# A sooner token list, and gathers in another order on GpSimd's queue, in a sorted feed-forward stage

## The chip, the cores and the metric

The kernel runs on one core of a Trainium2 chip. The metric is the device time of one execution in microseconds; below it is the median of three runs. A profile of one further execution stands beside it. Engines are named as the profile names them: PE is TensorE, DVE is VectorE, ACT is ScalarE, POOL is GpSimd, SP is the engine that issues plain transfers.

## What is computed

Four layers work on 2048 tokens of width 256 (8 sequences of 256). The change lies in the second, a hard-routed feed-forward. Each token walks down a binary tree of depth 8 and ends in one of 256 leaves; the leaf has its own small weights. Products q, k and v do this three times, with trees and weights of their own, on the same tokens:

```python
def _fff(x, nw, nb, w1, b1, w2, b2, act):
    node = jnp.zeros(x.shape[:2], dtype=jnp.int32)
    for _ in range(DEPTH):
        logit = jnp.einsum('bsd,bsd->bs', x, nw[node]) + nb[node]
        node = 2 * node + 1 + (logit > 0).astype(jnp.int32)
    leaf = node - NN
    h = act(jnp.einsum('bsd,bsdl->bsl', x, w1[leaf]) + b1[leaf])
    return jnp.einsum('bsl,bsld->bsd', h, w2[leaf]) + b2[leaf]

q = _fff(xn, q_nw, ...)
k = _fff(xn, k_nw, ...)
v = _fff(xn, v_nw, ...)
```

An attention over q, k and v, a fourth such product, and the other layers follow.

## The kernel before, in words

The function `group_products` handles q, k and v in one call (`nf` is 3, product number `f` is 0, 1, 2). It has two parts.

**Routing.** 24 items (8 blocks of 256 tokens for q, then for k, then for v) pass through a loop of 26 steps, `i` from 0 to 25, written out on PE and DVE. In step `i` PE computes the logits of item `i` (`pe_logits`, L1607), the leaf sums of item `i-1` (`pe_follow`, L1617) and the look-up of item `i-2` (`pe_look_up`, L1628). DVE turns logits into sides (`dve_sides`, L1567) and takes the look-up's result (`dve_take`). When a product's eight items are through, its tokens are sorted by leaf: `count` and `rank` on PE, `starts`, `slots`, `locate` on DVE, `find_tokens` on PE (L2209, it waits for the two halves of `is_row`, L2018), and `found_tokens` on DVE (its last instruction is L2034), which sets the semaphore `found_in`. From then on there is a list of the 2048 tokens in order of their leaves, and the row of the bias table for each. The step numbers at which q's pieces run are literals in the two loops (B is 8). `steps`, `words_of` and `pack` make the bits that say at which unit the group of leaves changes.

**Products.** The sorted tokens are 16 tiles of 128 (NT is 16), the leaves 32 groups of 8. A product is 47 units (UNITS), one for each pair of tile and group that can meet. A tile `t` is brought from the DRAM tensor `rows_x` by an indirect DMA on POOL's queue (`gather`, L1765) into one of six buffers (RING), is transposed by PE (`turn`, L2145 and L2147), and is copied by ACT to `xT`. A unit is `hidden` (L2158), ACT's activation, DVE's `leaf_only` (L2041), `output` (L2168), and DVE's `add` (L2060). The first `add` on a tile adds to rows of biases that another indirect DMA has put there (`seed`, L1778). In unit `u` PE does `turn` of tile `u+3` first; the turns of the next product's tiles 0 to 2 are done in units 44 to 46. So 16 turns lie in the first part of each product, and the last 34 units of each have none.

**POOL's queue.** POOL issues the gathers and seeds in program order and waits in that order. A gather of the `n`th tile in all (`n` is `16*f + t`) waits until turn `n-6` is done, because its buffer is that tile's, and until gather `n-2` has landed. A seed waits until the seed two before it has landed, and, for the third product, until the first product's tile has been stored. The order before is: six gathers, sixteen seeds, ten gathers for q; then for k and v each sixteen seeds and sixteen gathers.

**SP's queue.** While product `f` runs, SP loads the weights of product `f+1`, a pair of groups as the old pair is no longer needed (from unit 17 to the last), and stores each finished tile of product `f` (L1811, units 31 to 46). So SP's transfers are thickest at the end of q's and of k's units.

Of the kernel before, what the change touches and what calls it, by code (L numbers as in the profile page):

```python
# [1655 lines left out]
def group_products(core, name, first, nf, leaves, weights, places, rows, beside, gelu=False,  # L1656
# [5 lines left out]

    nc = core.nc
    RING = 6 if nf > 1 else NT
    HALF_K = 0.5 * (P - 1)
    with ExitStack() as own:
        def sb(n, shape, dt=F32):
# [85 lines left out]
        with nc.Block() as block:  # L1753
            @block.gpsimd
            def _(pool):
                def gather(f, t):

                    n = f * NT + t
                    if t == 0:
                        pool.wait_ge(found_in, f + 1)  # L1760
                    if n >= RING:
                        pool.wait_ge(x_ps, n - RING + 1)
                    if n >= 2:
                        pool.wait_ge(tile_in[(n - 2) % RING], 16 * ((n - 2) // RING + 1))
                    pool.indirect_dma_start(  # L1765
                        xs[n % RING][:], None, core.rows_x if route else core.rows_f,
                        bass.IndirectOffsetOnAxis(token_i[:, f, t:t + 1], 0)
                        ).then_inc(tile_in[n % RING], 16)

                def seed(f, t):  # L1770

                    if f == 1 and t == 0:
                        pool.wait_ge(route.G_sb, route.ITEMS)
                    if f > 1:
                        pool.wait_ge(stored[t], 16 * (f - 1))
                    if t >= 2:
                        pool.wait_ge(seeded[t - 2], 16 * (f + 1))
                    pool.indirect_dma_start(  # L1778
                        ys[f % 2][:, t * D:(t + 1) * D], None, core.dram["group_b2"],
                        bass.IndirectOffsetOnAxis(leaf_row[:, f, t:t + 1], 0)  # L1780
                        ).then_inc(seeded[t], 16)

                pool.iota(column_i[:], pattern=[[1, P]], base=0, channel_multiplier=0
                          ).then_inc(column_in, 1)
                if route:
                    route.pool(pool)
                    pool.wait_ge(route.rows_out, 16 * B)
                    for t in range(RING):
                        gather(0, t)
                    for t in range(NT):  # L1790
                        seed(0, t)
                    for t in range(RING, NT):
                        gather(0, t)
                    for f in range(1, nf):
                        for t in range(NT):
                            seed(f, t)
                        for t in range(NT):
                            gather(f, t)
                else:
                    pool.wait_ge(core.rows_out, 16 * B)  # L1800
                    for t in range(NT):
                        gather(0, t)
                    for t in range(NT):
                        pool.wait_ge(tile_in[t], 16)
                    beside.pool_ahead(pool)
# [95 lines left out]
            def _(dve):  # L1901
# [5 lines left out]
                def starts(f, k):  # L1907

                    if k == 0:
                        dve.wait_ge(counted, f + 1)  # L1910
                        dve.tensor_copy(run[0][:, LOW + 1:], psZ[:, 0:NG8 - 1]
                                        ).then_inc(count_in, 1)
                        dve.wait_ge(count_in, f + 1)
                    for n in ((0, 1), (2, 3, 4))[k]:
                        old, new = run[n % 2], run[1 - n % 2]
                        by = 1 << n
                        do(dve.tensor_tensor(new[:, LOW:], old[:, LOW:],
                                             old[:, LOW - by:LOW - by + NG8], ALU.add))
# [104 lines left out]
                def found_tokens(f):  # L2023

                    dve.wait_ge(found_ps, f + 1)
                    found = psZ[:, 0:3 * NT].rearrange("p (k t) -> p k t", k=3)
                    do.mark(dve.tensor_copy(sorted_leaf[:, f], found[:, 2]))
                    do(dve.tensor_copy(tile_row[:, 0], found[:, 0]))
                    do.mark(dve.tensor_tensor(token_i[:, f], tile_row[:, 0], found[:, 1], ALU.add))
                    do.mark(dve.tensor_tensor(  # L2030
                        leaf_row[:, f], sorted_leaf[:, f],
                        leaves.offset[:, first + f:first + f + 1].to_broadcast([P, NT]), ALU.add))
                    do.wait()
                    dve.tensor_copy(tile_row[:, 1, 0:1], tile_row[:, 0, 0:1]).then_inc(found_in, 1)  # L2034
# [29 lines left out]
                if route:  # L2064
                    route.dve_first(dve, do)
                    number_tokens()
                    for i in range(route.ITEMS + 2):
                        if i + 2 < B:
                            route.dve_normal(dve, i + 2)
                        if i < route.ITEMS:  # L2070
                            route.dve_sides(dve, i)
                        if i >= 2:
                            route.dve_take(dve, do, i - 2)
                        if i == B + 3:
                            starts(0, 0)
                        if i == B + 4:
                            starts(0, 1)
                        if i == B + 5:
                            slots(0, 0)
                        if i == B + 6:  # L2080
                            slots(0, 1)
                        if i == B + 7:
                            locate(0, 0)
                        if i == B + 8:
                            locate(0, 1)
                        if i == B + 9:
                            steps(0, 0)
                        if i == B + 10:
                            found_tokens(0)
                        if i == B + 11:  # L2090
                            steps(0, 1)
                        if i == B + 13:
                            pack(0)
                        if i == 2 * B + 3:
                            starts(1, 0)
                        if i == 2 * B + 4:
                            starts(1, 1)
                        if i == 2 * B + 6:
                            slots(1, 0)
                        if i == 2 * B + 7:  # L2100
                            slots(1, 1)
                        if i == 2 * B + 8:
                            locate(1, 0)
                        if i == 2 * B + 9:
                            locate(1, 1)
                else:
                    for k in range(2):
                        starts(0, k)
                    number_tokens()
                    for k in range(2):  # L2110
                        slots(0, k)
                    for k in range(2):
                        locate(0, k)
                    found_tokens(0)
                    for k in range(2):
                        steps(0, k)
                    pack(0)
# [18 lines left out]
            def _(pe):  # L2136
# [94 lines left out]
                if route:  # L2231
                    route.pe_turn(pe, 0)
                    for i in range(route.ITEMS + 2):
                        if i < route.ITEMS:
                            route.pe_logits(pe, i)
                        if i + 1 < B:
                            route.pe_turn(pe, i + 1)
                        if 1 <= i <= route.ITEMS:
                            route.pe_follow(pe, i - 1)
                        if i >= 2:  # L2240
                            route.pe_look_up(pe, i - 2)
                        if i == B + 3:
                            count(0)
                            rank(0)
                        if i == B + 9:
                            find_tokens(0)
                        if i == B + 12:
                            words_of(0)
                        if i == 2 * B + 3:
                            count(1)  # L2250
                        if i == 2 * B + 5:
                            rank(1)
                else:
                    count(0)
                    rank(0)
                    find_tokens(0)
                    words_of(0)
# [1371 lines left out]
```

## Time and profile before

| what | us |
|---|---|
| median of 3 runs | 1495.77 (1494.61 to 1495.92) |
| the profiled execution's own time | 1499.22 |
| its span in the profile | 1497.4 |
| PE busy in the span | 1241.3 |
| POOL busy in the span | 446.6 |
| first turn of q to last unit of v, about | 545 to 763 |

Times of the rows below are microseconds from the span's start. "Idle before" is the idle time of that engine just before an instruction, and behind the arrow is what ended it, as far as the profile shows; "issue" means nothing that it shows.

### The profile page before, as it was taken

Reading aid. Unit: us, or ns where it says so; the run is one execution under the profiler, and the core shown is the slowest. Engines: PE = TensorE matmul, PEld = TensorE weight load, DVE = VectorE, ACT = ScalarE, POOL = GpSimd, SP = SyncE. Lnnn points to the kernel's source line nnn. Section 1 sums busy time; section 2 is a strip of 40 time slices with the busy share of each in tenths; the row PEclk is TensorE's granted clock in tenths of the full one; section 3 lists DMA queues with packets and bytes.
Section 4 is the critical chain, followed back from the end, with each engine's and each line's share of the span. In section 5 each row is a group of like instructions: output and inputs, shape, how many; then the busy total and the mean of one; then the engine's idle time right before and its main releaser. Section 6 shows DMA issues by size and latency. Waiting matters only on the chain. (4 is left out here: it accounts for less than half of the span.)

```text
span 1497.4 us, 24672 instructions
## 1 busy us (share of the span) xinstructions
PE 1241.3 (83%) x7232; PEld 900.6 (60%) x7236; DVE 885.1 (59%) x2513; ACT 582.4 (39%) x1106; POOL 446.6 (30%) x588
## 2 busy tenths in 40 slices
PE   1298999999875866888957758779999889999997
PEld 1195777777664755666646636556676555555554
DVE  8998999999514654645533455554656424453534
ACT  2124556665421224465632316344555541212110
POOL 2258344544461055243225416432111000000000
PEclk9658999999988988998977879887999989999999
DMA  9000000000003623759154505630100000000000
GB/s 274 0 2 2 1 1 1 1 1 1 1 1 60 245 74 92 232 162 299 48 174 146 177 27 117 157 81 8 16 9 8 1 1 0 15 0 14 0 15 14
DMA packets 85380, 92.70 MB, mean 62 GB/s; under 512 B 19400, under 2 KB 70090, under 8 KB 85260
## 3 DMA queue, kind: packets, MB, share of 16 engines
q1 hardware_dynamic: 72972, 66.05, 14.0%
q0 software_dynamic: 12288, 25.18, 6.8%
q8 instruction: 60, 0.98, 0.3%
q14 instruction: 60, 0.49, 0.1%
HBM read 76.51 MB, written 14.68 MB: 61 GB/s over the span
## 5 line engine op out<-in xcount | busy, mean ns | idle before, releaser
L3350 ACT ACTIVATE m_silu<-m_psG 128x512 f32<-128x512 f32 x48 | 28.7, 597 | 215.2 <-PE m_psU L3470 215.2
L2158 PE MATMUL gq_psH<-gq_xT,gq_w 128*128 (+1 forms) x564 | 101.1, 305 | 10.7 <-ACT gq_xT L1852 3.7
L3403 DVE TENSOR_TENSOR m_act<-m_silu,m_psU 128x512 f32<-128x512 f32 x48 | 33.0, 688 | 122.4 <-ACT m_silu L3350 107.7
L2158 PEld LDWEIGHTS gq_psH<-gq_xT,gq_w 128*128 128x128 f32 x564 | 80.9, 205 | 37.6 <-issue 32.9
L2041 DVE SCALAR_TENSOR_TENSOR gq_hT<-gq_xT,unit_leaf,gq_act 128x128 f32<-128x128 f32 x141 | 49.7, 352 | 78.5 <-ACT gq_act L1873 36.7
L2168 PE MATMUL gq_psY<-leaf_w,gq_hT 128*128 (+1 forms) x282 | 90.9, 405 | 6.2 <-DVE gq_hT L2041 4.3
L3470 PE MATMUL m_psG<-m_xnT,m_gate 128*128 128x512 f32 x192 | 91.8, 601 | 2.1 <-PEq L192 2.1
L3470 PE MATMUL m_psU<-m_xnT,m_up 128*128 128x512 f32 x192 | 90.8, 595 | 0.0
L1765 POOL DMA_INDIRECT gq_x<-rows_x,gq_token_i x48 | 46.0, 958 | 127.6 <-DVE gq_tile_row L2034 61.9
L765 DVE MATCH_REPLACE8 s_product_a_rest<-a_top,s_product_a_rest 128x256 f32<-128x256 f32 x192 | 76.1, 408 | 0.3 <-issue 0.3
L2764 ACT ACTIVATE c_probT<-c_psA 128x2048 f32<-128x2048 f32 x32 | 60.1, 1878 | 33.2 <-PE c_psA L3058 33.2
L205 POOL TENSOR_SCALAR m_rstd<-m_mean_var 128x4 f32<-128x4 f32 x4 | 0.9, 231 | 240.2 <-DVE m_mean_var L1297 240.2
L2060 DVE TENSOR_TENSOR gq_y<-gq_psY,gq_y 128x256 f32 (+1 forms) x141 | 59.6, 423 | 21.9 <-PE gq_psY L2168 13.4
L2867 DVE TENSOR_REDUCE c_max<-c_psA 128x4 f32<-128x1024 f32 x32 | 39.2, 1226 | 49.6 <-PE c_psA L3024 49.6
L3482 PE MATMUL m_psD<-m_down,m_act 128*128 128x256 f32 x256 | 60.9, 381 | 7.1 <-DVE m_acc L3428 7.1
L3428 DVE SCALAR_TENSOR_TENSOR m_acc<-m_psD,m_weight,m_acc 128x256 f32<-128x256 f32 x128 | 53.1, 478 | 22.3 <-PE m_psD L3482 22.3
L755 DVE MAX8 a_top<-s_product_a_rest 128x8 f32<-128x256 f32 x192 | 64.9, 411 | 2.0 <-DVE s_product_a_rest L765 0.5
L1873 ACT ACTIVATE gq_act<-gq_psH,leaf_b 128x128 f32<-128x128 f32 x141 | 51.4, 365 | 36.8 <-PE gq_psH L2158 22.6
L3470 PEld LDWEIGHTS m_psU<-m_xnT,m_up 128*128 128x128 f32 x192 | 36.9, 192 | 46.7 <-issue 46.7
L3482 PEld LDWEIGHTS m_psD<-m_down,m_act 128*128 128x128 f32 x256 | 48.1, 190 | 25.6 <-issue 14.2
L1058 PE MATMUL a_psW<-s_tables_a_work,a_w 128*128 128x256 f32 x256 | 60.6, 393 | 2.7 <-ACT s_tables_a_work L663 2.7
L1865 ACT ACTIVATE gq_w<-leaf_w 128x256 f32 (+1 forms) x141 | 58.2, 413 | 4.7 <-issue 4.3
(545 smaller groups left out, 3093.0 us busy)
## 6 DMA issues: line engine op xcount, KB each, us to landing
leaf_w<-in_group_w SPq DMA_DIRECT2D x128, 128.0 KB
leaf_w<-in_group_w SPq DMA_DIRECT2D x64, 256.0 KB
a_w<-in_L_xattn_W SPq DMA_DIRECT2D x2, 1024.0 KB, 12.9
rows_x<-token_rows SPq DMA_DIRECT2D x8, 256.0 KB, 5.1
sorted_y_q<-gq_y SPq DMA_DIRECT2D x16, 128.0 KB
sorted_y_k<-gq_y SPq DMA_DIRECT2D x16, 128.0 KB
sorted_y_v<-gq_y SPq DMA_DIRECT2D x16, 128.0 KB
rows_f<-token_rows SPq DMA_DIRECT2D x8, 256.0 KB
```

Of the source, the lines that this page charges most:

```text
L755: do.mark(dve.max(top[:, j, 8 * r:8 * r + 8], row_in(r, j)))
L765: last = dve.match_replace(rest[:, j, :], top[:, j, 8 * r:8 * r + 8], row_in(r, j), NEG_TAKEN)
L1058: last = pe.matmul(pW[:, 2 + c // 2 % 2, c % 2, :], w1[:, k, c * P:(c + 1) * P], hT[:, k, :], start=(k == 0), stop=(k == DC - 1))
L1865: act.activation(w1[n % 3][:], weights.w1[:, :, bass.ds(g * P, P)], ACT.Copy).then_inc(w_sb, 1)
L1873: act.activation(act_h[n % 2][:], psH[n % 2][:, 0:P], ACT.Gelu if gelu else ACT.Relu, bias=weights.b1[:, first + f, bass.ds(g, 1)]).then_i ...
L2060: dve.tensor_tensor(here, psY[n % 3][:, 0:D], here, ALU.add).then_inc(y_sb, 1)
L2158: last = pe.matmul(psH[n % 2][:, 0:P], w1[n % 3][:, c, :], xT[:, c, bass.ds(g * -P + u * P, P)], start=(c == 0), stop=(c == DC - 1))
L2168: pe.matmul(psY[n % 3][:, 0:D], hT[n % 2][:], weights.w2[:, bass.ds(g * D, D)], start=True, stop=True).then_inc(y_ps, 1)
L2764: act.activation(probT[c][:], psA[:], ACT.Exp, scale=float(DH1) ** -0.5).then_inc(exps.s, 1)
L3428: last = dve.scalar_tensor_tensor(acc[:, t, :], psD[:, t, :], wt[:, t, e:e + 1], acc[:, t, :], ALU.mult, ALU.add)
L3470: last = pe.matmul(o[u % 2][:], w[:, u, c, :], xnT[:, c, :], start=(c == 0), stop=(c == DC - 1))
L3482: last = pe.matmul(psD[:, t, :], act_u[u % 2][:, t * P:(t + 1) * P], down[:, u, :], start=True, stop=True)
```

## The change

Two things are done. First, q's sorting pieces are put at earlier routing steps and closer together: `count` and `rank` at step B+2 (was B+3) and before that step's look-up, both parts of `starts` at B+2, of `slots` at B+3 and of `locate` at B+4 (were B+3 to B+8, one a step), `find_tokens` at B+5 (was B+9), `found_tokens` at B+6 (was B+10), `steps` at B+7 and B+8, `words_of` at B+9, `pack` at B+10.

Second, POOL's order is the same for each product now: six gathers, nine seeds, then gather and seed by turns (gathers 6 to 12, seeds 9 to 15), then gathers 13 to 15. Every gather or seed waits for the one issued two before it, of whichever kind.

```diff
+    SEEDS = 9
...
-                    if n >= 2:
-                        pool.wait_ge(tile_in[(n - 2) % RING], 16 * ((n - 2) // RING + 1))
+                    if len(under_way) >= 2:
+                        pool.wait_ge(*under_way[-2])
+                    under_way.append((tile_in[n % RING], 16 * (n // RING + 1)))
...
-                    if t >= 2:
-                        pool.wait_ge(seeded[t - 2], 16 * (f + 1))
+                    pool.wait_ge(*under_way[-2])
+                    under_way.append((seeded[t], 16 * (f + 1)))
...
-                    for t in range(RING):
-                        gather(0, t)
-                    for t in range(NT):
-                        seed(0, t)
-                    for t in range(RING, NT):
-                        gather(0, t)
-                    for f in range(1, nf):
-                        for t in range(NT):
+                    for f in range(nf):
+                        for t in range(RING):
+                            gather(f, t)
+                        for t in range(SEEDS):
                             seed(f, t)
-                        for t in range(NT):
+                        for t in range(SEEDS, NT):
+                            gather(f, t - SEEDS + RING)
+                            seed(f, t)
+                        for t in range(NT - SEEDS + RING, NT):
                             gather(f, t)
...
+                        if i == B + 2:
+                            starts(0, 0)
+                            starts(0, 1)
                         if i == B + 3:
-                            starts(0, 0)
+                            slots(0, 0)
+                            slots(0, 1)
                         if i == B + 4:
-                            starts(0, 1)
-                        if i == B + 5:
-                            slots(0, 0)
+                            locate(0, 0)
+                            locate(0, 1)
                         if i == B + 6:
-                            slots(0, 1)
+                            found_tokens(0)
...
+                        if i == B + 2:
+                            count(0)
+                            rank(0)
                         if i >= 2:
                             route.pe_look_up(pe, i - 2)
-                        if i == B + 3:
-                            count(0)
-                            rank(0)
+                        if i == B + 5:
+                            find_tokens(0)
                         if i == B + 9:
-                            find_tokens(0)
-                        if i == B + 12:
                             words_of(0)
```

## Rows read from the trace of the kernel before

**Rows 1.** The page's first line.

```profile
span 1497.4 us, 24672 instructions
```

**Rows 2.** Stretch, length; PE, PEld, DVE, ACT, POOL busy us; PEclk, DMA share, GB/s.

```profile
545.10:582.00 36.90, 25.24 (x150) 19.43 (x151) 13.61 (x44) 13.74 (x38) 22.17 (x23) 0.81 0.27 83
634.60:662.00 27.40, 22.29 (x139) 16.95 (x137) 10.71 (x31) 15.81 (x45) 12.43 (x13) 0.99 0.54 170
694.70:730.30 35.60, 27.79 (x141) 19.83 (x141) 11.43 (x32) 16.06 (x46) 14.75 (x16) 0.86 0.58 183
```

**Rows 3.** PE's waits from 500 to 775 us: total, times, longest.

```profile
PE gq_psX L2145 <- DMA gq_x<-rows_x,gq_token_i: 15.1, 9, 8.9
PE gq_psX L2145 <- issue: 9.1, 6, 5.4
```

**Rows 4.** PE's timeline: start, length, line, operation, turns, and k's last output.

```profile
545.09 0.66 PE L2145 MATMUL gq_psX<-identity,gq_x 128*128 128x128 f32 x2 [2.85 <-issue]
...
581.14 0.38 PE L2145 MATMUL gq_psX<-identity,gq_x 128*128 128x128 f32 x2
...
634.64 0.38 PE L2145 MATMUL gq_psX<-identity,gq_x 128*128 128x128 f32 x2
...
640.60 0.38 PE L2145 MATMUL gq_psX<-identity,gq_x 128*128 128x128 f32 x2
...
661.36 0.48 PE L2145 MATMUL gq_psX<-identity,gq_x 128*128 128x128 f32 x2
...
694.11 0.63 PE L2168 MATMUL gq_psY<-leaf_w,gq_hT 128*128 x2
700.11 0.66 PE L2145 MATMUL gq_psX<-identity,gq_x 128*128 128x128 f32 x2 [5.36 <-issue]
...
729.57 0.44 PE L2145 MATMUL gq_psX<-identity,gq_x 128*128 128x128 f32 x2 [0.60 <-DMA gq_x<-rows_x,gq_token_i]
```

**Rows 5.** POOL's timeline: seeds of q, gathers of q, gathers of k.

```profile
553.04 0.94 POOL L1778 DMA_INDIRECT gq_y<-in_group_b,gq_row_leaf  x1 [0.80 <-DMA gq_y<-in_group_b,gq_row_leaf]
...
555.94 0.94 POOL L1778 DMA_INDIRECT gq_y<-in_group_b,gq_row_leaf  x1 [0.70 <-DMA gq_y<-in_group_b,gq_row_leaf]
...
569.89 0.94 POOL L1765 DMA_INDIRECT gq_x<-rows_x,gq_token_i  x1 [2.66 <-DMA gq_x<-rows_x,gq_token_i]
...
573.35 0.95 POOL L1765 DMA_INDIRECT gq_x<-rows_x,gq_token_i  x1 [1.27 <-PE gq_psX L2147]
...
635.40 0.95 POOL L1765 DMA_INDIRECT gq_x<-rows_x,gq_token_i  x1 [17.02 <-PE gq_psX L2147]
...
641.63 0.94 POOL L1765 DMA_INDIRECT gq_x<-rows_x,gq_token_i  x1 [4.03 <-PE gq_psX L2147]
...
648.06 0.94 POOL L1765 DMA_INDIRECT gq_x<-rows_x,gq_token_i  x1 [3.92 <-PE gq_psX L2147]
```

**Rows 6.** Busy time by stretch, around the first gathers of k's ring.

```profile
636.00:648.00 12.00, 10.20 (x68) 8.00 (x65) 5.61 (x16) 7.54 (x23) 3.18 (x4) 1.00 0.82 286
648.00:656.00 8.00, 7.10 (x44) 5.38 (x45) 2.83 (x8) 5.22 (x15) 4.85 (x5) 1.00 0.23 66
```

**Rows 7.** Routing: DVE's busy time in three plain steps, and in five with q's list.

```profile
496.70:503.80 7.10, 7.10 (x50) 6.03 (x49) 4.17 (x18) 2.06 (x3) 0.00 (x0) 1.00 1.06 375
504.90:521.10 16.20, 14.47 (x104) 11.91 (x102) 14.39 (x54) 4.16 (x7) 0.00 (x0) 1.00 0.43 149
```

**Rows 8.** Routing: timelines of PE (logits), DVE (the list's end) and SP (last `rows_x`).

```profile
509.25 1.97 PE L1607 MATMUL gq_psH<-gq_y,gq_xT 128*128 128x256 f32 x8
...
521.40 3.61 PE L1607 MATMUL gq_psH<-gq_y,gq_xT 128*128 128x256 f32 x8
...
525.44 1.97 PE L1607 MATMUL gq_psH<-gq_y,gq_xT 128*128 128x256 f32 x8
...
527.01 0.15 DVE L2034 COPY gq_tile_row<-gq_tile_row 128x1 f32<-128x1 f32 x1
...
508.10 0.43 SPq L1500 DMA_DIRECT2D rows_x<-token_rows  x1
```

More of the change, by code:

```diff
@@ L1755, in _ @@
             def _(pool):
+                under_way = []
                 def gather(f, t):
@@ L2073, in _ @@
                             route.dve_take(dve, do, i - 2)
+                        if i == B + 2:
+                            starts(0, 0)
+                            starts(0, 1)
                         if i == B + 3:
-                            starts(0, 0)
+                            slots(0, 0)
+                            slots(0, 1)
                         if i == B + 4:
-                            starts(0, 1)
-                        if i == B + 5:
-                            slots(0, 0)
+                            locate(0, 0)
+                            locate(0, 1)
                         if i == B + 6:
-                            slots(0, 1)
+                            found_tokens(0)
                         if i == B + 7:
-                            locate(0, 0)
+                            steps(0, 0)
                         if i == B + 8:
-                            locate(0, 1)
-                        if i == B + 9:
-                            steps(0, 0)
+                            steps(0, 1)
                         if i == B + 10:
[L2089 to L2092, printed above, removed]
                             pack(0)
```

## The prediction

> **What bounds the kernel now.** I read the page's first line for the span [rows 1], then PE's waits, then busy time by stretch, then the timelines of PE and POOL. The products follow each other on PE, and what comes after them waits for v's last unit, so a microsecond gained or lost on PE in the products moves the end by as much. In the 218 us of the products PE's largest wait is for gathered tiles: 15.1 us in nine waits, and 9.1 us more that the profile puts down to nothing but which lie at the same instruction, the first transpose of a turn [rows 3]. All of that is in the part of each product that has turns. These parts, from first to last turn, are the three stretches of [rows 2]. PE is busy 25.2 of 36.9 us in q's, 22.3 of 27.4 in k's, and 27.8 of 35.6 in v's. The last 34 units of each product have no turns and don't depend on POOL. So I cost the change by three windows and move the rest bodily. A window runs from when PE could begin turn 0 to the start of turn 15 [rows 4]:
>
> q: 581.14 - 545.09 = 36.05. k: 661.36 - 634.64 = 26.72. v: PE is through with what precedes at 694.11 + 0.6 = 694.7 and waits 5.36 us, so 729.57 - 694.7 = 34.9. Together 97.7 us. A window has 16 turns; k's, the shortest, gives 1.8 us a turn, so PE could hardly do any of them in less than 26 us.
>
> **What the change does to a window.** Before, q's window contained the last seeds and ten gathers, k's only ten gathers, because k's sixteen seeds had been issued while q's turnless units ran, in time that POOL otherwise idles: it waits 17.02 us before k's gather 6 [rows 5]. Now gather 6 of a product can't be issued before that product's turn 0 is done (its buffer), and seven seeds stand behind it in the queue, each ahead of the next gather. So each window now contains 17 POOL transfers, ten gathers and seven seeds, and PE's turns 7 to 15 wait for them. No instruction is added or removed on any engine; the waits and the order are all.
>
> POOL's chain in a window is then: gather 6 about 0.9 us after turn 0 begins (k's: 635.40 against 634.64, [rows 4, 5]); from a gather to the next one is one pair, gather and seed, and the next gather waits for the last one's landing; from gather 6 to 13 are seven pairs, from 13 to 15 one more; gather 15 needs about 3.0 us to reach PE (estimate: the landing time of the pairs below). With p for a pair: 0.9 + 8p + 3.0.
>
> What p is: two transfers are in flight at once, so a pair lasts from one issue to its landing. Two seeds in quiet time: 555.94 - 553.04 = 2.9, 2.95 in the mean of the neighbours. Two gathers in quiet time: 573.35 - 569.89 = 3.46 [rows 5]; other late gathers show the same. I take 3.2, in the middle, since both kinds go by turns now; the ends are 2.95 and 3.46. Near the start of k's window a pair is much longer: 641.63 - 635.40 = 6.2 and 648.06 - 641.63 = 6.4. The profile names PE as the releaser of both, but the turns that these gathers need are 2 and 4 of k, and even turn 4 was done by 641.3 (it began at 640.60, [rows 4]); what came last was the landing of the gather two before. That is SP's burst: the DMA engines are 0.82 busy from 636 to 648, at 286 GB/s, and 0.23 from 648 to 656 [rows 6]. The burst is tied to the last units of the product before, so it stays where it is relative to turn 0, for k and for v. Before, ten gathers could bear two slow pairs: PE had tiles 0 to 5 in hand and the two pairs served tiles 6 to 9. Now the two slow pairs bring only tiles 6 and 7.
>
> The Trainium skill (DMA: Bandwidth & Descriptors, section Latency and other measured facts) gives the memory's latency as 0.2 us in the mean and 2 us at high load, a dominant part of a transfer's fixed cost. The trace agrees in direction, and shows more: 6.2 against 3.46 us. By the page's 1.8 us on top of 3.2 the two slow pairs would be 5.0 each, and the sum below would be +0.7 instead of +5.9.
>
> **q.** Window 0.9 + 8 x 3.2 + 3.0 = 29.5 us; SP is silent here, so no slow pair. The sooner list is what lets six gathers and nine seeds (15 x 1.5 = 22.5 us at two in flight) be out of the way by turn 0. Before, it was ready at 527.01 [rows 8], too late for that. Now: the list needs 14.39 - 5 x 4.17/3 = 7.4 us of DVE [rows 7], and 7.4 us in three PE steps of 2.36 us (7.1 us for three in the plain stretch, [rows 7]), of which plain routing takes 1.39 each, is 4.5 us too much. `find_tokens` stands on PE one step behind `locate` and waits for it, with the logits of the next item behind it. Before, the same meeting cost 521.40 - (509.25 + 4 x 2.36 = 518.7) = 2.7 us, and 1.6 us for logits at half the clock after it (3.61 against 1.97) [rows 8]. So PE comes out of routing about 2 us later than before, with 0 and +4 as ends; the list comes at about 519 to 520, and the rows of tokens in DRAM, last issued at 508.10, are long there. 520.5 + 22.5 = 543 is ahead of turn 0 at 547. If PE's loss were hidden the term would be 0; nothing lies over it, since PE paces routing.
>
> **k.** 0.9 + 6.2 + 6.4 + 6 x 3.2 + 3.0 = 35.7. **v.** The same, and 0.7 more: six gathers after k's last turn and nine seeds under SP's loads take about as long as k's 34 turnless units (33.3 us), so gather 6 may come 0 to 1.5 us late. 36.4. The 5.36 us before v's turn 0 are gone in return, since v's first gathers are no longer behind sixteen seeds; that is inside the 34.9 of before.
>
> **Sum.** 2.0 + 29.5 + 35.7 + 36.4 = 103.6 against 97.7: +5.9 us. By window: q -4.5, k +9.0, v +1.5. With p at 2.95: 2.0 + 27.5 + 34.2 + 34.9 = 98.6, +0.9; at 3.46: 2.0 + 31.6 + 37.3 + 38.0 = 108.9, +11.2. The windows were read in an execution that took 1499.22 us with a span of 1497.4; the median of the runs shown is 1495.77, and I put the difference on that: 1501.7.
>
> **Rivals.** *The burst does not meet POOL's chain.* POOL issues nothing now between its fifteen early transfers and k's gather 6; SP's loads may drain further ahead, and all pairs be 3.2. For it: in 648 to 656 the engines are at 0.23. Against it: 286 GB/s in the 12 us where the slow pairs lie come from SP's own stores and loads [rows 6]. Then 2.0 + 29.5 + 29.5 + 30.2 = 91.2, -6.5, 1489.3: faster. It decides when a slow pair costs under 1.5 us more than a quiet one, about half of what was read.
>
> *One slow pair a window instead of two*, if the burst is shorter by some 4 us: 2.0 + 29.5 + 32.5 + 33.2 = 97.2, -0.5, 1495.3: no change. For it: fewer of POOL's own transfers are in the engines before it.
>
> *Worse.* p at 3.46, a third slow pair (+3 in k and v), routing +4: 4 + 31.6 + 40.3 + 41.0 = 116.9, +19; or PE, waiting in every turn, falls to its lower clock for the units behind a window, as for the logits at 521.40 [rows 8]. Half of this is likelier than all: 1507 to 1512.
>
> *It doesn't do what it says*: the list is sooner but the first turn isn't, as turn 0 waits for all of routing. That is so, and is in the sum; a sooner list alone gives nothing but room for the seeds.
>
> **How the numbers follow.** Forecast 0.47, by itself 1496.7 to 1507; one slow pair 0.17; no slow pair 0.18; worse 0.18. About 0.2% (3 us) is what a measurement of this kernel can tell from no change. Slower: 0.18 and all but 0.05 of 0.47, 0.60. Same: 0.17 + 0.05 = 0.22. Faster: 0.18. The range reaches from the better case to the milder half of the worse: 1490 to 1508.
>
> **What would show it.** Right: `found_in` near 519; turn 0 of q at 547; turn 15 of q 27 to 32 us later; k's turn 15 34 to 37 us behind its turn 0 (was 26.7), with waits for gathered tiles from turn 7 on; no wait of 5 us before v's turn 0; two pairs over 5 us on POOL after turn 0 of k and of v. Wrong: k's window under 32 us, or a pair p outside 2.9 to 3.5 in quiet time, or seeds late enough that DVE's `add` waits.

## The result, and the profile after

The changed kernel takes 1506.65 us (median of six runs, 1501.25 to 1512.45), the kernel before 1495.19 beside it (six runs, 1490.16 to 1499.56). The ratio is 1.0079, 95% interval 1.0049 to 1.0108: slower, by 11.5 us between the medians. The profiled execution of the changed kernel is its fastest, 1501.25 us, so its span is only 2.0 us over [rows 1]:

```profile
span 1499.4 us, 24679 instructions
```

The loss has to be looked for in the products, and there it is whole. PE's timeline after, the turns that answer to [rows 4] (turn 0 and 15 of q, then k's turn 0, 6, 7 and 15, then v's turn 0, 6 and 15):

```profile
545.07 0.66 PE L2145 MATMUL gq_psX<-identity,gq_x 128*128 128x128 f32 x2 [2.69 <-DVE token_rows L1577]
...
579.18 0.38 PE L2145 MATMUL gq_psX<-identity,gq_x 128*128 128x128 f32 x2
...
629.07 0.38 PE L2145 MATMUL gq_psX<-identity,gq_x 128*128 128x128 f32 x2
...
642.11 0.44 PE L2145 MATMUL gq_psX<-identity,gq_x 128*128 128x128 f32 x2 [3.16 <-DMA gq_x<-rows_x,gq_token_i]
...
645.66 0.69 PE L2145 MATMUL gq_psX<-identity,gq_x 128*128 128x128 f32 x2 [1.44 <-DMA gq_x<-rows_x,gq_token_i]
...
667.45 0.38 PE L2145 MATMUL gq_psX<-identity,gq_x 128*128 128x128 f32 x2
...
699.47 0.38 PE L2145 MATMUL gq_psX<-identity,gq_x 128*128 128x128 f32 x2
...
711.52 0.69 PE L2145 MATMUL gq_psX<-identity,gq_x 128*128 128x128 f32 x2 [3.47 <-DMA gq_x<-rows_x,gq_token_i]
...
741.18 0.63 PE L2145 MATMUL gq_psX<-identity,gq_x 128*128 128x128 f32 x2
```

The windows are q 34.11 us, k 38.38, v 41.71: together 114.2 where they were 97.7. Between the windows the turnless units take 49.89 and 32.02 us, where they took 53.50 and 33.3: 4.9 us less. v's last turn is thus at 741.18 instead of 729.57, 11.6 us later. The two profiles end only 2.0 us apart because what follows (the attention and the fourth product, which the change doesn't touch) took 758.2 us in this execution and 767.8 in that of before. The medians differ by 11.5 us, as v's last turns do, so I put the difference in what follows down to the two executions; the other profile of the changed kernel (e10 below) has 767.5 us there.

PE's waits over the stretch from 515 to 765 us:

```profile
PE gq_psX L2145 <- DMA gq_x<-rows_x,gq_token_i: 23.5, 19, 3.5
```

Before, 15.1 us were put down to the transfers and 9.1 to "issue" [rows 3]. Now there are 19 short waits, one in nearly every late turn, and none of "issue". The prediction took all 9.1 for waits for tiles; 2.85 of them stand before q's turn 0 [rows 4], where the changed kernel has 2.69 put down to routing's `token_rows`. Busy time by stretch, for the windows of q, k and v and, third, for k's turnless units (columns as in [rows 2]):

```profile
545.00:579.00 34.00, 28.50 (x148) 21.91 (x149) 13.37 (x44) 14.22 (x40) 18.55 (x19) 0.71 0.24 70
...
629.00:667.00 38.00, 28.81 (x136) 22.04 (x134) 10.99 (x30) 15.23 (x44) 17.10 (x18) 0.69 0.43 133
667.00:699.00 32.00, 31.72 (x196) 24.44 (x196) 24.14 (x64) 24.32 (x67) 11.54 (x12) 1.00 0.78 250
699.00:741.00 42.00, 32.03 (x139) 24.42 (x139) 11.41 (x32) 15.89 (x45) 18.08 (x19) 0.65 0.50 161
```

PE has the same work in k's window as before, spread over 38 us instead of 27.4, and its mean granted clock is 0.69 where it was 0.99 [rows 2]: with a wait in every turn it spends much of the window at 1.2 GHz instead of 2.4. POOL's timeline shows what the turns wait for (L1769 is a gather, L1782 a seed; the first pair is q's, then come k's, then v's):

```profile
550.64 0.94 POOL L1769 DMA_INDIRECT gq_x<-rows_x,gq_token_i  x1 [1.39 <-DMA gq_x<-rows_x,gq_token_i]
551.89 0.95 POOL L1782 DMA_INDIRECT gq_y<-in_group_b,gq_row_leaf  x1 [0.30 <-issue]
554.11 0.94 POOL L1769 DMA_INDIRECT gq_x<-rows_x,gq_token_i  x1 [1.27 <-PE gq_psX L2147]
...
603.16 0.94 POOL L1782 DMA_INDIRECT gq_y<-in_group_b,gq_row_leaf  x1 [1.66 <-DMA gq_y<-in_group_b,gq_row_leaf]
629.84 0.94 POOL L1769 DMA_INDIRECT gq_x<-rows_x,gq_token_i  x1 [25.73 <-PE gq_psX L2147]
...
636.34 0.94 POOL L1769 DMA_INDIRECT gq_x<-rows_x,gq_token_i  x1 [4.30 <-DMA gq_x<-rows_x,gq_token_i]
...
642.81 0.94 POOL L1769 DMA_INDIRECT gq_x<-rows_x,gq_token_i  x1 [4.28 <-PE gq_psX L2147]
...
646.36 0.94 POOL L1769 DMA_INDIRECT gq_x<-rows_x,gq_token_i  x1 [1.27 <-DMA gq_x<-rows_x,gq_token_i]
...
699.13 0.95 POOL L1782 DMA_INDIRECT gq_y<-in_group_b,gq_row_leaf  x1 [3.98 <-DMA gq_y<-in_group_b,gq_row_leaf]
700.60 0.95 POOL L1782 DMA_INDIRECT gq_y<-in_group_b,gq_row_leaf  x1 [0.53 <-issue]
705.47 1.06 POOL L1769 DMA_INDIRECT gq_x<-rows_x,gq_token_i  x1 [3.92 <-DMA gq_y<-in_group_b,gq_row_leaf]
...
712.22 0.94 POOL L1769 DMA_INDIRECT gq_x<-rows_x,gq_token_i  x1 [4.39 <-DMA gq_y<-in_group_b,gq_row_leaf]
```

Three things are to be seen. A quiet pair lasts 3.47 us (550.64 to 554.11). POOL is through with k's 15 early transfers at 604.1 and then idles 25.73 us until k's turn 0 lets it go on; before, it idled 17.02 there [rows 5], with seven more seeds done. And in v it never idles: its nine early seeds go at the pace of SP's loads, and gather 6 comes 6.0 us after turn 0 (705.47 against 699.47).

### The profile page after: what moved, and what is told of

The parts are those of the page before. It is cut to its first block and busy times, and to the rows that moved or that the text cites. A ratio compares the mean times of both kernels' runs of the same rounds, so it can differ in the third digit from the quotient of the medians.

```text
span 1499.4 us, 24679 instructions
## 1 busy us (share of the span) xinstructions
PE 1255.8 (84%) x7236; PEld 913.7 (61%) x7236; DVE 885.2 (59%) x2513; ACT 582.6 (39%) x1106; POOL 445.9 (30%) x588
## 5 line engine op out<-in xcount | busy, mean ns | idle before, releaser
L2158 PE MATMUL gq_psH<-gq_xT,gq_w 128*128 (+1 forms) x564 | 107.1, 319 | 4.4 <-ACT gq_w L1868 3.1
L2158 PEld LDWEIGHTS gq_psH<-gq_xT,gq_w 128*128 128x128 f32 x564 | 87.8, 220 | 28.3 <-issue 23.5
L2168 PE MATMUL gq_psY<-leaf_w,gq_hT 128*128 (+1 forms) x282 | 99.0, 437 | 5.9 <-DVE gq_hT L2044 5.8
L1769 POOL DMA_INDIRECT gq_x<-rows_x,gq_token_i x48 | 46.8, 975 | 141.3 <-DVE gq_tile_row L2037 53.9
```

What stands on the lines that cost most here:

```text
L2158: last = pe.matmul(psH[n % 2][:, 0:P], w1[n % 3][:, c, :], xT[:, c, bass.ds(g * -P + u * P, P)], start=(c == 0), stop=(c == DC - 1))
L2168: pe.matmul(psY[n % 3][:, 0:D], hT[n % 2][:], weights.w2[:, bass.ds(g * D, D)], start=True, stop=True).then_inc(y_ps, 1)
```

## The experiments

All times are medians beside the kernel before on the same chip. The ratio with its interval is a measure of its own and not the quotient of two medians: in e7 the medians give 0.991 and the ratio is 0.993. Each row of the table comes from one execution. Within a group the runs shared a chip; the groups (e1b to e4b, e5 to e7, e8 to e10, e11 and e12) were on different chips, on which the kernel before itself had 1497.83, 1502.61, 1495.11 and 1503.23 us. The table gives what the profile of each shows: the start of q's turn 0, the three quantities that turned out to matter (k's window, the turnless units between q's and k's windows, and the time from k's last turn to v's), and v's last turn.

| kernel | q turn 0 | q window | q to k | k window | k's last to v's last | v's last | ratio |
|---|---|---|---|---|---|---|---|
| before | 545.09 | 36.05 | 53.50 | 26.72 | 68.2 | 729.57 | 1 |
| changed | 545.07 | 34.11 | 49.89 | 38.38 | 73.7 | 741.18 | 1.0079 |
| e1b list alone | 550.72 | 33.73 | 49.36 | 24.34 | 71.6 | 729.75 | 0.9986 |
| e2b order alone | 543.14 | 40.63 | 47.88 | 36.87 | 72.0 | 740.50 | 1.0113 |
| e3b three in flight | 559.08 | 34.33 | 57.19 | 37.31 | 79.5 | 767.36 | 1.0340 |
| e4b weights of k, v left out | 547.14 | 33.96 | 47.99 | 33.24 | 67.1 | 729.45 | 1.0003 |
| e5 two in flight alone | 541.20 | 37.84 | 52.21 | 23.84 | 73.3 | 728.34 | 0.9993 |
| e6 list, two in flight | 550.15 | 26.34 | 51.89 | 24.94 | 72.9 | 726.19 | 0.9937 |
| e7 16 seeds early | 546.66 | 27.63 | 47.90 | 25.36 | 72.2 | 719.74 | 0.9932 |
| e8 16, 16, 9 seeds | 544.91 | 28.88 | 47.75 | 24.58 | 73.1 | 719.20 | 0.9997 |
| e9 as e7, list late | 545.19 | 39.14 | 47.19 | 26.60 | 73.9 | 732.03 | 1.0006 |
| e10 the changed one again | 543.85 | 34.36 | 47.16 | 38.11 | 74.8 | 738.25 | 1.0092 |
| e11 as e7, again | 550.28 | 26.79 | 47.26 | 26.25 | 72.7 | 723.25 | 0.9907 |
| e12 as e8, again | 548.64 | 25.56 | 48.03 | 24.67 | 72.5 | 719.39 | 0.9916 |

**The list alone (e1b).** The routing steps of the change, with POOL's order and waits as before.

```diff
+                        if i == B + 5:
+                            find_tokens(0)
                         if i == B + 9:
-                            find_tokens(0)
...
+                        if i == B + 6:
+                            found_tokens(0)
...
-                        if i == B + 10:
-                            found_tokens(0)
```

> The sooner list alone, with POOL's queue in the order of the kernel before. Theory (POOL's chain in each window sets PE's turns): the list is there at about 519 instead of 527, so q's gather 6 moves from 561.5 to about 553 and q's turn 15 from 581 to about 573; k's and v's windows stay at 26.7 and 34.9 us. 8 us faster than before, 1487 for 1495. Rival (the compressed routing costs PE, and turn 0 comes later): the gain is smaller by 2 us or more. Rival (the changed kernel's loss comes from the list): slower than before.

1494.01 us (12 runs), 0.9986 [0.9957, 1.0016]: no difference that can be told. The sooner list does no harm by itself, and the 8 us that were expected of it did not come. q's gather 6 was issued at 551.87, as expected (553), and its last one at 568.92. But turn 0 was at 550.72, and q's turn 15 at 584.45 instead of 573: behind the gathers ACT stood idle three times in waits that the profile calls "remote" and that no semaphore of the program ended. ACT's timeline has one such wait in routing and one in q's window:

```profile
533.57 0.69 ACT L1520 ACTIVATE r_leaf<-gq_psY,minus_margin 128x512 bf16<-128x512 f32 x1 [4.36 <-remote]
...
574.09 0.49 ACT L1853 ACTIVATE gq_xT<-gq_psX 128x384 f32<-128x384 f32 x1 [4.17 <-remote]
```

From 515 to 600 us they add up to 24.8 us on ACT, where the changed kernel, with two in flight, has none; e6 and e7 below, also with two, have 5.8 and 3.0. So the rival that turn 0 comes later holds as well.

**The order alone (e2b).** The other half: POOL's new block, the rule of two in flight with it, the list where it was.

```diff
+    SEEDS = 9
...
-                    for t in range(RING):
-                        gather(0, t)
...
+                    for f in range(nf):
+                        for t in range(RING):
+                            gather(f, t)
```

> POOL's new order alone, with the list at its old steps. Theory: k's window 38 and v's 42 us as in the changed kernel (from 26.7 and 34.9), less the few microseconds gained between windows; q's fifteen early transfers end at about 550 instead of 545, so q's turn 15 is 3 to 5 us later than in the changed kernel. 13 to 17 us slower than before. Rival (order is harmless, list guilty): within 3 us of before.

1512.37 us (6 runs), 1.0113 [1.0074, 1.0152]. The new block is the whole loss, by 14.5 us (13 to 17 expected): k's window is 36.87 us, and v's last turn at 740.5, as in the changed kernel. e5 below has the rule of two in flight alone and loses nothing, which leaves the order.

**Three in flight (e3b).**

```diff
-                    if len(under_way) >= 2:
-                        pool.wait_ge(*under_way[-2])
+                    if len(under_way) >= 3:
+                        pool.wait_ge(*under_way[-3])
```

> The changed kernel with three transfers in flight instead of two. Theory (a pair lasts as long as one transfer's landing because only two are in flight): a transfer every 1.25 us in quiet time, so pairs of 2.5 instead of 3.5; slow pairs 4 to 5 instead of 6.4; v's nine seeds are out before v's turn 0. Windows near 27, 31 and 32 instead of 34.1, 38.4 and 41.7: some 20 us faster than the changed kernel, 5 to 10 faster than before. Rival (the transfers share one server, and more in flight only lengthens each): no change against the changed kernel, landing times grow from 3.5 to 5 us.

1548.06 us, 1.034 [1.0294, 1.0387]: 50 us slower than before and 37 slower than the changed kernel by the ratios (1.034 against 1.009), where a gain was expected. POOL's timeline, first and seventh transfer of q and the fifteenth, shows that it now issues one every 1.25 us and waits for nothing:

```profile
520.46 1.25 POOL L1769 DMA_INDIRECT gq_x<-rows_x,gq_token_i  x1 [54.47 <-DVE gq_tile_row L2037]
...
528.28 0.94 POOL L1782 DMA_INDIRECT gq_y<-in_group_b,gq_row_leaf  x1 [0.30 <-issue]
...
538.28 0.95 POOL L1782 DMA_INDIRECT gq_y<-in_group_b,gq_row_leaf  x1 [0.30 <-issue]
```

And ACT's timeline shows "remote" idle time as in e1b, one of 9.22 us ending 2.7 us after POOL's last transfer of that row:

```profile
532.00 0.69 ACT L1520 ACTIVATE r_leaf<-gq_psY,minus_margin 128x512 bf16<-128x512 f32 x1 [6.08 <-remote]
...
541.91 0.69 ACT L1520 ACTIVATE r_leaf<-gq_psY,minus_margin 128x512 bf16<-128x512 f32 x1 [9.22 <-remote]
...
679.39 0.49 ACT L1855 ACTIVATE gq_xT<-gq_psX 128x384 f32<-128x384 f32 x1 [7.47 <-remote]
```

Turn 0 of q is 14 us late by this, before any window, and v's last turn is 37.8 us behind that of the kernel before. So in this kernel the transfers' latency is not to be bought off with a third in flight. A possible cause is that the transfers that bring the engines their instructions (the page's part 3 has them on queues 8 and 14: 60 packets each in the changed kernel) don't get through; from 515 to 560 us this kernel's trace has 3 such packets and the changed kernel's 5, though fewer packets can as well follow from engines that stand still. The Trainium skill (DMA: Bandwidth & Descriptors, section Queues, rings and completion order) keeps row 14 of the queues for the runtime, refill among its uses. That fits the packets on queue 14, and no run here shows that the stalled engines were out of instructions. It is argued, not shown.

**SP's weights left out (e4b).** The changed kernel, with k's and v's leaf weights loaded for 8 columns of each part instead of all: the kernel leaves out most of these weights, and its results for k and v are not those of the reference.

```diff
-                    weights.load_pair(sp, first + f, j)
+                    weights.load_sliver(sp, first + f, j)
...
+        for c in range(DC):
+            sp.dma_start(self.w1[:, c, pair * GH:pair * GH + 8],
+                         rows[:, c * GH:c * GH + 8]).then_inc(self.pair_in[pair], 16)
```

> The changed kernel with k's and v's leaf weights not loaded: each of their transfers carries 32 bytes a row instead of up to 2 KB (so k and v use mostly q's weights). Theory (SP's loads make the slow pairs and v's late seeds): k's window 38.4 to about 33, v's 41.7 to about 32, in all 12 to 15 us faster than the changed kernel. Rival (the slow pairs come from the stores, or from the turn of the product itself): under 4 us.

1497.78 us, 1.0003 [0.9972, 1.0035], where the changed kernel has 1.008 to 1.009: 11 to 13 us by the ratios, where 12 to 15 were expected, and the rival allowed 4. POOL's timeline behind k's turn 0, gathers 6 to 9:

```profile
629.85 0.95 POOL L1779 DMA_INDIRECT gq_x<-rows_x,gq_token_i  x1 [26.39 <-PE gq_psX L2157]
...
633.62 0.94 POOL L1779 DMA_INDIRECT gq_x<-rows_x,gq_token_i  x1 [1.57 <-PE gq_psX L2157]
...
637.37 0.94 POOL L1779 DMA_INDIRECT gq_x<-rows_x,gq_token_i  x1 [1.55 <-PE gq_psX L2157]
...
640.84 0.94 POOL L1779 DMA_INDIRECT gq_x<-rows_x,gq_token_i  x1 [1.04 <-PE gq_psX L2157]
```

3.77 and 3.75 us a pair instead of 6.50 and 6.47: SP's loads are what makes these pairs slow, 5.4 us in k's window (which is 5.1 shorter). From k's last turn to v's it saves 6.6 us; v's window is 34.7 us, where 32 was expected. What is left, k's window of 33.24 against 26.72, is the seeds at quiet speed.

**Two in flight with the old list and order (e5).** The trace of before has up to four transfers in flight where gathers and seeds meet, and idle times behind those places that the profile puts down to nothing but "issue" (26.4 us at DVE's `hT`, 10.3 at ACT's `xT`); the change's rule takes that away as a by-effect, and I took this for the source of the 4.9 us between the windows.

```diff
-                    if n >= 2:
-                        pool.wait_ge(tile_in[(n - 2) % RING], ...)
+                    if len(under_way) >= 2:
+                        pool.wait_ge(*under_way[-2])
...
-                    if t >= 2:
-                        pool.wait_ge(seeded[t - 2], 16 * (f + 1))
+                    pool.wait_ge(*under_way[-2])
```

> The kernel before with one thing changed: a transfer of POOL waits for the last but one transfer before it, whichever kind it is, so that never more than two are on their way; before, up to four are where gathers and seeds meet. Theory (four in flight at a crossing is what leaves ACT, DVE and PE idle for nothing the program shows, and puts v's first turn 5.4 us behind PE's free time): turn 0 of v moves from 700 to about 695, the ACT and DVE idles put down to issue or remote behind the crossings (10.3 us at ACT, 26.4 us at DVE before) go, and the time is 4 to 8 us under before. Rival (the crossings cost nothing on the way to the end): the time is that of before within 2 us, and v's first turn stays near 700.

1499.11 us, 0.9993 [0.9963, 1.0024]. The theory falls. DVE still has 20.0 us of "issue" and "remote" at `hT`, and v's turn 0 is still late, put down to "issue" by PE's timeline, although only two were in flight:

```profile
698.46 0.66 PE L2148 MATMUL gq_psX<-identity,gq_x 128*128 128x128 f32 x2 [10.94 <-issue]
```

POOL's timeline of the same kernel tells what it waited for. v's last seed and its first gather are

```profile
692.77 0.94 POOL L1781 DMA_INDIRECT gq_y<-in_group_b,gq_row_leaf  x1 [2.48 <-DMA gq_y<-in_group_b,gq_row_leaf]
695.61 0.94 POOL L1768 DMA_INDIRECT gq_x<-rows_x,gq_token_i  x1 [1.90 <-DMA gq_y<-in_group_b,gq_row_leaf]
```

The first gather was issued at 695.61, behind sixteen seeds under SP's loads, and turn 0 began 2.85 us later. "issue" hid a plain wait for a transfer.

**The list and the rule, old order (e6); 16 seeds instead of nine (e7).** e6 has the new list and two in flight, with the order of before. e7 is one number: every product's six gathers, then all sixteen seeds, then ten gathers.

```diff
-    SEEDS = 9
+    SEEDS = 16
```

> The changed kernel's earlier token list and its rule of two in flight, with the order of the kernel before (q: six gathers, 16 seeds, ten gathers; k and v: 16 seeds, then 16 gathers). Theory (the list and the rule are gains, only the order is the loss): q's first turn at 545 and its turns in 28 to 31 us instead of 36.1, k's in 25 to 28 and v's in 30 to 35; 10 to 15 us under before. Rival one (the earlier list does nothing, because the 32 transfers of q are what they were and the list start is 4 us sooner at best): 2 to 5 us under before, all of it from the rule. Rival two (the early transfers hit the routing work as in the run of the list alone): turn 0 of q at 550 and the time of before.

> The changed kernel with SEEDS 16 instead of 9: each product's six gathers first, then its 16 seeds, then ten gathers alone. Theory (the cost of the change is that seven seeds lie between the gathers that PE waits for, at 3.5 us a pair where a gather alone takes 1.7): q as in the run with the old order, k's and v's last ten gathers come every 1.7 to 2 us once PE takes them, but only if the 16 seeds are through by the first turn; in k POOL is free for them, so k's turns take 25 to 28 us instead of 38.4; in v, where SP's loads slow the seeds to 5 to 6 us late for nine of them, 16 seeds would be 15 to 18 us late and v's turns take 40 or more. Sum: 5 to 12 us under the changed kernel, 0 to 6 over before. Rival (the order within a product doesn't matter, the 32 transfers per product are the bound however they are laid): the time of the changed kernel within 3 us.

e6: 1493.04 us, 0.9937 [0.9906, 0.9968]. e7: 1488.52 us, 0.9932 [0.9902, 0.9961], the kernel before at 1502.61 beside both. Both are faster than the kernel before, and by the ratios than the changed one, which did not run on this chip. e6 gains 9.5 us, a little under the 10 to 15 expected, with q's turn 0 at 550.15 and not at 545. The sooner list (e1b) and the rule (e5) do nothing measurable alone and 0.6% together. The smaller "remote" idle time on ACT (5.8 us against e1b's 24.8) may be why; that is argued from one profile each. e7 came out better than expected, under before and not 0 to 6 us over it: v's last turn is 9.8 us sooner, because q's window is 8.4 us shorter, the units behind it 5.6 and k's window 1.4, against 4.0 more from k's last turn to v's and 1.6 from turn 0. With no seed in the window, k's takes 25.36 us in e7 (theory 25 to 28) and q's 27.63. PE's timeline of e7, k's first and last turn and v's turn 0, 6 and 15:

```profile
622.19 0.38 PE L2145 MATMUL gq_psX<-identity,gq_x 128*128 128x128 f32 x2
...
647.55 0.44 PE L2145 MATMUL gq_psX<-identity,gq_x 128*128 128x128 f32 x2 [0.57 <-DMA gq_x<-rows_x,gq_token_i]
...
679.58 0.38 PE L2145 MATMUL gq_psX<-identity,gq_x 128*128 128x128 f32 x2
...
703.74 0.69 PE L2145 MATMUL gq_psX<-identity,gq_x 128*128 128x128 f32 x2 [15.58 <-DMA gq_x<-rows_x,gq_token_i]
...
719.74 0.44 PE L2145 MATMUL gq_psX<-identity,gq_x 128*128 128x128 f32 x2
```

k's window has PE at full clock again (busy time by stretch of e7):

```profile
622.00:648.00 26.00, 22.55 (x140) 16.86 (x138) 11.26 (x32) 15.79 (x45) 10.48 (x11) 1.00 0.56 183
```

v loses in one wait of 15.58 us what its late gathers win. That led to the next question, whether v's order matters at all.

**Nine seeds in v alone (e8), the late list with 16 seeds (e9), the changed kernel again (e10).**

```diff
-    SEEDS = 9
+    SEEDS = (16, 16, 9)     # e8, by product
+    SEEDS = 16              # e9, and the list's steps of before
```

> SEEDS 16 for q and k, 9 for v. Theory (POOL's total is what counts: from k's last gather to v's last, POOL has no idle time that isn't a wait for a landing, 71 to 73 us for 32 transfers in any order, so v's order is without effect, and the seven seeds cost only where POOL stood idle ahead of a first turn, as in k): the time of the run with 16 everywhere within 3 us, v's last turn at 717 to 723; only v's gather 6 comes sooner, and the turns after it are spaced 3.5 us. Rival (nine are better where seeds are slow, or the pairs cost in v too): v's last turn 5 us or more away from 719.7, in either direction.

> The kernel before's routing steps (token list at 526 instead of 520) with the six gathers first, 16 seeds, ten gathers of every product and two in flight. Theory (q's transfers run back to back from the list on, so the list's lead is passed on whole): q's last turn 3 to 6 us later than in the run with 16 and the early list, 1492 to 1496 against 1488.5. Rival (the list's lead is lost in idle time before k's first turn, or q's end is set by its first turn): 1488 to 1490, q's last turn at 574 to 576.

> The changed kernel itself, beside the others on their chip. 10 to 13 us over before, 16 to 20 over the run with 16 seeds in k.

e8: 1493.3 us, 0.9997 [0.9979, 1.0016]. Its profile does what the theory says: v's gather 6 comes 5.0 us behind turn 0 instead of 21.4 (turn 6 at 688.58 instead of 703.74), and v's last turn is at 719.20 against 719.74. But its time was not that of e7. e9: 1497.0, 1.0006 [0.9985, 1.0027]. That is 3.7 us over e8 on the same chip by the medians and 1.3 by the ratios, whose intervals overlap. In the profiles q's last turn is 10.5 us later than e8's (584.33 against 573.79), where 3 to 6 were expected. The list's lead is passed on in the profiles, and its worth in time is not measured. e10: 1508.8, 1.0092 [1.0062, 1.0123], k's window 38.11 us and v's last turn at 738.25; that is 13.7 us over before and 15.5 over e8 (10 to 13 and 16 to 20 expected).

**e7 and e8 once more, together (e11, e12).**

> The kernel with 16 seeds everywhere once more, now beside the one with (16, 16, 9): the first came out at 0.9932 of before on one chip, the second at 0.9997 on another, though their profiled runs agree to 1 us in every turn. Theory (they are equal, both about 0.4% faster than before, and the difference was the chips'): ratio 0.993 to 0.998, the two within 3 us. Rival (v's order matters after all): 4 to 6 us between the two.

> SEEDS (16, 16, 9) on the same chip: theory 0.993 to 0.998 of before, within 3 us of the one with 16 everywhere; rival 4 to 6 us over it. v's last turn at 717 to 723 in both.

e11: 1488.86 us, 0.9907 [0.9876, 0.9938]. e12: 1489.18 us, 0.9916 [0.9889, 0.9943]. They are equal, and both gain more than the 0.993 to 0.998 expected. What differs is the kernel before: 1503.23 us on this chip and 1495.11 on that of e8. So the sooner list with the seeds out of the windows is faster than before by 0.7 to 0.9% on two chips, and on a third it could not be told from it; why the chips differ in this stays open.

## Why the prediction was right, and where its terms were not

**The mechanism.** The forecast was +5.9 us, because k's and v's windows contain seven seeds now, each ahead of a gather that PE waits for. It held: the order alone is 1.0113, and one number that takes the seeds out of the windows turns the changed kernel's k window from 38 us to 25 and its ratio from 1.009 to 0.993. On one and the same chip e8, with the seeds out of q's and k's windows, is 15.5 us under the changed kernel (e10). The time fell at 1506.65, inside the range, at the upper edge of the forecast's own (1496.7 to 1507), but the change cost 11.5 us and not 5.9. Four terms were off: q by 2.6 us, k by 2.7, v by 5.3, and the units between the windows by 4.9 the other way. That the last one hid nearly half of the others is luck: without it the time would have been about 1511.5, outside the range.

Of the signs named in advance, the list at 519, k's waits from turn 7 on, its two slow pairs and the missing wait before v's turn 0 came. q's and k's windows were longer than their 27 to 32 and 34 to 37 us, q's turn 0 was at 545 and not 547, and v had one slow pair and not two. A quiet pair was 3.47 us, at the upper end of what was allowed.

**k: +9.0 forecast, +11.7 measured.** By the formula, k's window is 0.8 to the first gather, 6.50 and 6.47 for two slow pairs, 21.0 for six pairs, 3.7 for the last gather to reach PE. The slow pairs were 6.2 and 6.4 in the forecast, so nearly right; e4b shows that SP's burst makes them. The estimate that the prediction weighed from the latency figure of the Trainium skill (DMA: Bandwidth & Descriptors, section Latency and other measured facts) would have made them 5.0 and the window 33: the measurement decides against it here. The term that was mis-sized is p, 3.5 instead of 3.2, which makes 1.8 of the 2.7 us; the last gather's way to PE makes another 0.7. I took the mean of a pair of gathers (3.46) and of seeds (2.95). But with the kinds by turns a gather always waits for the transfer two before it, which is the last gather, and the seed between goes out 0.30 us after POOL is free: a mixed pair lasts as long as the slower kind, and no mean is to be taken. The rows for this stood in [rows 5].

**v: +1.5 forecast, +6.8 measured** (41.71 against 34.9). I let nine seeds under SP's loads end about when PE is ready, 0 to 1.5 us late; they ended 6.0 late. One slow pair follows instead of two. The step behind it was the wrong picture of v. Under SP's full loads POOL is never ahead in v. From k's last turn to v's last turn it takes 71.6 to 74.8 us in every profile of the table but three, whichever order v's 32 transfers have (the three: before with 68.2, e3b, and e4b with its 67.1 by lighter loads). What v's order gains at turn 0 (32 us of turnless units instead of 43.4 in e5) it gives back at gather 6 (15.58 us in e7). Thus v mostly inherits k's delay. How much it adds is not settled: the changed kernel's 73.7 us are 5.5 more than the 68.2 in the one profile of the kernel before, but within 2.1 of the 71.6 to 73.3 of e1b, e5 and e6, whose v has the old order too.

**q: -4.5 forecast, -1.9 measured.** The window shrank to 34.11, not 29.5: eight pairs at 3.5 instead of 3.2 are 2.4 us of it, the first of them took 4.43, and the last gather needed 4.1 us to reach PE instead of 3.0. Turn 0 was expected 2.0 us later and was not later in the result's profile; but over all profiles with the sooner list (nine, e3b aside) turn 0 is at 543.85 to 550.72, mean 547.5, and with the late list (four) at 541.20 to 545.19, mean 543.7. So the expected cost of 2 us, with its ends of 0 and 4, was rather too small, and one profile told otherwise. The same kernel had 546.66 in e7 and 550.28 in e11: a term of this size isn't to be read from one execution.

**Between the windows: 0 forecast, -4.9 measured.** I moved the turnless units bodily. From q's last turn to k's first it takes 47.2 to 49.9 us in the kernels with six gathers first (e3b aside), 51.9 to 53.5 in before, e5 and e6 with k's seeds first, but 49.4 in e1b. Two in flight isn't the cause (e5). An influence of the order is likely; by what way is open.

**The rivals.** No slow pair: wrong, k has both and v one. Worse, by PE's clock: the clock fell to 0.69 and 0.65, but within the windows, where PE waits anyway; k's window is fully accounted for by POOL's chain, and the units behind k's window ran at 1.00, those behind v's at 0.97. DVE's timeline has the list's last instruction at 519.17, as forecast (519 to 520; before 527.01, [rows 8]), and PE's has `find_tokens` waiting on `is_row` and the logits behind it:

```profile
519.17 0.15 DVE L2037 COPY gq_tile_row<-gq_tile_row 128x1 f32<-128x1 f32 x1
```

```profile
512.32 0.36 PE L2209 MATMUL gq_psZ<-gq_ids,gq_is_row 128*128 128x48 bf16 x8 [3.02 <-DVE gq_is_row L2021]
...
513.65 3.56 PE L1607 MATMUL gq_psH<-gq_y,gq_xT 128*128 128x256 f32 x8
```

That is the 3.0 us of wait and 1.6 us of slow logits that the prediction took over from the old meeting. No wait of DVE's `add` for seeds appeared.

## What to carry to other kernels

Count, for each stretch, the transfers that a queue must do between the first use and the last, and put there only those that can't go earlier: a transfer in the queue's idle time (25.7 us before k's turn 0) is free, the same one between two gathers that are waited for costs its full share, here 13 us for seven. Where two kinds go by turns with two in flight, price the pair by the slower kind. Where the queue never idles, as in v, its order had no effect on the end (e7 against e8, e11 against e12), and an early first tile is paid back at a later one.

## What the runs showed of the hardware

Two indirect transfers of 128 rows in flight took 3.47 us a pair in quiet and 6.5 under SP's loads; with the loads cut to slivers, 3.75. With a third in flight POOL issued every 1.25 us, but ACT and DVE stood idle for 6 to 9 us at a time with no releaser that the profile shows, and the kernel took 3.4% longer than before. And idle time that the profile puts down to "issue" may be a wait for a transfer: PE's 10.94 us ended when v's first gather, issued 2.85 us earlier, could have landed.
